# A linear-attention stream that ran inside the first of two layers' iterations is laid over both layers, two iterations to a block of 128 tokens

## What is computed

```python
# linear attention ("mix"): 16 heads of 32
vp = ln(x) @ W_in;  v, p = split(vp);  q = ln(x) @ Wq + bq;  k = ln(x) @ Wk + bk
q = softmax(q);  k = softmax(k);  k = (1 - smear) * k + smear * k_prev      # k_prev: the token before
attn = tril((q / s) @ (k / s).T * decay);  o = attn @ v / (attn.sum(-1) + eps)
s_out = ln(silu(p) * o @ W_out)
# two layers of windowed attention (8 heads of 64, windows of 128) and a gated MLP
h = shift_token(x);  q, k, v = split(h @ wqkv)
q, k = rotary(l2norm(q), l2norm(k));  x = x + softmax(q k^T over this window and the last) v @ wo
h = ln(shift_token(x));  a, g = split(h @ w1 + b1);  x = x + (a * gelu(g)) @ w2 + b2
# end: silu of the second layer's output times s_out, plus x
```

## Time and profile before

| | |
|---|---|
| median of 3 runs | 2132.61 us (2131.91 to 2133.89) |
| profiled execution: time, span | 2133.59 us, 2131.8 us |
| PE busy, DVE busy | 1949.6 us, 1823.7 us |
| ACT busy, POOL busy | 1148.5 us, 935.3 us |
| granted TensorE clock, mean | 0.983 |

### The profile page before, as it was taken

One profiled execution on the slowest core, in us unless ns is written; L12 is line 12 of the kernel. 1 busy time (PEld: TensorE's weight loads), 2 busy tenths in 40 slices (PEclk: granted clock), 3 DMA queues, 4 the chain that ended last, 5 costly groups with the idle time before them and its releaser, 6 DMA issues.

```text
span 2131.8 us, 48702 instructions
## 1 busy us (share of the span) xinstructions
PE 1949.6 (91%) x15282; PEld 1672.7 (78%) x15282; DVE 1823.7 (86%) x5354; ACT 1148.5 (54%) x2734; POOL 935.3 (44%) x941
## 2 busy tenths in 40 slices
PE   4889999989989999999999999899999999999997
PEld 2777878878878778787787887788788788888886
DVE  5688998998998999999899899778888888888884
ACT  2334544544553553554454454656776776676673
POOL 2444554554564465455455455323333333333331
PEclk8799999999999999999999999999999999999998
DMA  5000000000000000000000001121111111111110
GB/s 181 12 15 24 21 18 17 21 20 18 21 20 16 23 20 16 23 20 16 21 17 20 18 22 46 40 70 31 37 37 30 37 36 31 37 33 33 37 29 26
DMA packets 71792, 64.37 MB, mean 30 GB/s; under 512 B 12444, under 2 KB 64984, under 8 KB 71608
## 3 DMA queue, kind: packets, MB, share of 16 engines
q1 hardware_dynamic: 71736, 63.65, 9.9%
HBM read 38.45 MB, written 12.58 MB: 24 GB/s over the span
## 4 chain that ended last, share of the span: by engine, by line
PE 44%; DVE 34%; issue 15%; DMA 3%; ACT 1%; DVEq 1%; SPq 1%; POOL 1%; POOLq 0%; ACTq 0%
PE bank L1327 31%; PE bank L1332 7%; PE bank L1339 5%; DVE prob L942 5%; DVE prob L928 4%; DMA x_shift<-x 3%; DVE rot L1252 3%; DVE sq_sum L1198 2%; DVE qk_sum L1211 2%; DVE rot L1230 2%; DVE hid L1259 1%; DVE state L975 1%; DVE v_mix L1225 1%; DVE h_n L1160 1%; DVE h_n L1158 1%
## 5 line engine op out<-in xcount | busy, mean ns | idle before, releaser
L1327 PE MATMUL bank<-hT_n,w_s 128*128 128x128 f32 x3072 | 390.9, 279 | 0.5 <-ACT hT_n L713 0.5
L1327 PEld LDWEIGHTS bank<-hT_n,w_s 128*128 128x128 f32 x3072 | 366.1, 193 | 15.2 <-issue 10.8
L1332 PE MATMUL bank<-wqkv_s,xT 128*128 128x512 f32 x1152 | 318.8, 412 | 23.7 <-DVE xT L1106 18.5
L743 ACT ACTIVATE prob<-prob,row_min 128x256 f32<-128x256 f32 x512 | 256.1, 503 | 64.4 <-DVE row_min L928 62.0
L1332 PEld LDWEIGHTS bank<-wqkv_s,xT 128*128 128x128 f32 x1152 | 207.4, 191 | 81.7 <-DVE xT L1106 27.0
L942 DVE TENSOR_SCALAR prob<-prob,row_inv 128x256 f32<-128x256 f32 x512 | 224.4, 480 | 9.2
L928 DVE CUSTOM_DVE_ANT_0 prob<-bank,table,inv_norm 128x256 f32<-128x256 f32 x512 | 226.1, 478 | 2.0 <-issue 2.0
L635 POOL TENSOR_TENSOR rot_other<-raw,rot_t 128x256 f32<-128x256 f32 x256 | 186.7, 762 | 93.2 <-ACT raw L713 93.2
L598 POOL TENSOR_TENSOR inv_norm<-sq_clip,half_neg 128x16 f32<-128x16 f32 x64 | 188.7, 2948 | 63.6 <-DVE sq_clip L1201 63.6
L1327 PE MATMUL bank<-w_s,hid 128*128 128x256 f32 x768 | 206.5, 386 | 0.2 <-DVE hid L1259 0.2
L1339 PE MATMUL bank<-table,prob 128*128 128x128 f32 x1024 | 159.7, 279 | 42.6 <-DVE prob L942 40.4
(11 more groups left out here) (182 smaller groups left out, 4361.7 us busy)
## 6 DMA issues: line engine op xcount, KB each, us to landing
k_prev<-k_carry SPq DMA_DIRECT2D x32, 224.0 KB, 2.5
x_s<-in_L_attn_x SPq DMA_DIRECT2D x32, 128.0 KB, 2.1
rot_s<-in_rotary SPq DMA_DIRECT2D x64, 64.0 KB, 2.0
s_between_passes<-s_out SPq DMA_DIRECT2D x32, 128.0 KB, 1.7
x_between_layers<-x SPq DMA_DIRECT2D x32, 128.0 KB, 1.7
x_s<-x_between_layers SPq DMA_DIRECT2D x32, 128.0 KB, 2.0
xn<-x_between_layers SPq DMA_DIRECT2D x32, 128.0 KB, 2.1
s_out<-s_between_passes SPq DMA_DIRECT2D x32, 128.0 KB, 2.1
```

The lines of the kernel that those rows point to most:

```text
L743: ins = act.activation(prob[:, h, :], prob[:, h, :], ACT.Exp, bias=row_min[:, c:c + 1], scale=-1.0, accum_out=row_sum[:, c:c + 1])
L1327: return pe.matmul(out, lhsT, rhs, start=first, stop=last)
L1332: ins = pe.matmul(out, halved(left[:, a]), halved(right[:, b]), start=first and n == 0, stop=last and n == 2)
```

## The change

The mix is spread over all 64 iterations. `linear(i)` gives three pieces: in an odd iteration `one` (chunk i//2: transposes of the rows, q, k, v, p, softmaxes, smear, transposes of k and q at the iteration's end) and `y` (the last norm's output of the chunk before); in an even one `two` (scores, decays, values, state, output product of the chunk whose `one` ran in the iteration ahead). The normalised rows of all windows are stored to DRAM as they are made (`store_rows`, `xh_d`) and read back a chunk at a time (`x_mix`, in the buffer of `y_n`). Score banks 2 and 3 are now the two `mlp_bank`; `turn_q` and `turn_k` use `proj_bank` in both layers, so every `proj_bank_free` waits for kl; the output projection always uses `att_bank[1]`. POOL's `root` for `inv_norm` stands ahead of the two scalings of k. In layer 1 the closing product works in other buffers, and SP waits for the last store of it ahead of loading `x_in`.

The set-up is in two parts: identity, `wqkv`, rotary scales and the first rows are loaded first, and iteration 0 starts on them; the mix weights are prepared inside iteration 0 (`set_up_mix` on PE behind the v product, `cut_mix` on ACT behind the square and on DVE at the iteration's end), and the first chunk's transposes, in iteration 1, wait for the end of it (`mlp_cols`). `fold` writes to `mlp_bank[0]`.

```diff
+        def linear(i):
+            odd, n = i.c == 1, i.low // 2
+            return (Chunk(i.k, n) if odd and n < NW else None,
+                    Chunk(i.k - 1, n - 1) if not odd and 1 <= n < NW + 1 else None,
+                    Chunk(i.k - 1, n - 1) if odd and 1 <= n < NW + 1 else None)
...
-        score_bank = [mix_bank[0], mix_bank[1], att_bank[0], att_bank[2]]
+        score_bank = [mix_bank[0], mix_bank[1], mlp_bank[0], mlp_bank[1]]
...
+            def store_rows(n):
+                sp.wait_ge(norm_dve.sem, norm_dve.at("xh", n))
+                sp.dma_start(xh_d[row(n), :], xh[:, :]).then_inc(xh_stored, 16)
...
+                if i.c == 0 and i.low < UNITS:
+                    c = Chunk(i.k, i.low // 2)
+                    sp.wait_ge(xh_stored, 16 * (c.number() + 1))
+                    sp.dma_start(x_mix[:, :], xh_d[rows, :]).then_inc(xmix_loaded, 16)
...
# POOL, body
+                if two is not None:
+                    pool.wait_ge(mix_act.sem, mix_act.at("qt", two))
+                    pool.tensor_tensor(qT_dec[:, :, :], qT_mix[:, 0:MG // 2, :], query_decay,
...
# DVE, body (layer 0 and 1)
+                if two is not None:
+                    dve.wait_ge(mix_pool.sem, mix_pool.at("gate", two))
+                    decay_scores(two, 3)
                 if a is not None:
                     weigh("a1", a)
+                if two is not None:
+                    decay_scores(two, 2)
+                if a is not None:
                     weigh("b0", a)
...
+                if a is not None:
                     scores("b1", a, att_bank[0])
+                if two is not None:
+                    decay_scores(two, 0)
+                    dve.wait_ge(mix_pool.sem, mix_pool.at("kdec", two))
+                    decay_scores(two, 1)
...
+                if i.low == 0:
+                    cut_mix()
...
# PE, body
+                if one is not None:
+                    pe.wait_ge(xmix_loaded, 16 * (one.number() + 1))
+                    if one.low == 0:
+                        pe.wait_ge(setup_dve.sem, setup_dve.at("mlp_cols", ONCE))
+                    transposes(mix_bank[0], [x_mix[:, c * P:(c + 1) * P] for c in range(DC)])\
...
                 if a is not None:
                     pe.wait_ge(att_act.sem, att_act.at("tb1", a))
                     pe.wait_ge(att_dve.sem, att_dve.at("la", a))
                     att_values("b", a, att_bank[1])
+                if u is not None:
+                    turn_q(u)
+                if m is not None:
+                    hidden(m, mlp_bank[0], 2, 4, 2).then_inc(mlp_pe.done("ga"), 1)
+                    mlp_out(m, 0, 2)
+                if a is not None:
+                    out_projection(a, att_bank[1])
```

More of the change, by code:

```diff
@@ L761, in body @@
             def body(i):
-                mix, proj, a, m, f = streams(i)
+                proj, a, m, f = streams(i)
+                one, two, y = linear(i)
                 if i.low in QKV_CUT:
```

681 lines of the change are left out of this document (334 added, 347 removed).

## The result

The changed kernel takes **2190.02 us** (median of 4 runs, 2189.73 to 2191.0) against 2132.68 for the kernel before (4 runs): ratio **1.0269**, 95% interval 1.0251 to 1.0287. It is slower, by 57 us; I had said 2109 and a range up to 2165. The sign and the range are wrong.

What follows compares the result with a forecast made beforehand. PE was taken to lead, DVE close behind. 110 to iteration 3, 920 to iteration 31, 1021 for 32 to 63, 12 for the change of layers and 46 at the end gave 2109 to 2110 us; range 2055 to 2165.

Steps and rivals of the forecast that it cites:

- the second of the new waits: Even iterations: PE waits for decays standing among DVE's weighings; 1.05 us together, bounds 0 and 1.6.
- step (4): Layer 1's odd iterations: closing product ahead of weigh b1 costs PE 1.3 us, bounds 0.6 and 3; iteration 31.2.
- the work of PE in the base: Layer 1's iteration of 22.94 us, less 0.49 and about 0.5 of waits: 21.9, with xT's 0.36 still in it.
- The check against 15.5: PE's mix work: 7.0 + 8.6 = 15.6 us against 37.44 - 21.97 = 15.5 from the old windows.
- (1) `turn_q`: Query transposes wait for ACT's copy of v: 1.0 us in every iteration of both layers, kept at 0.7 to 1.1.
- (3) layer 0's odd iterations: DVE is the longer engine there: 30.9 us an iteration, bounds 29.9 and 31.7.
- POOL's order: Root ahead of k's scalings: 1.7 us less for weigh b1, later steps meet scalings and gate; counted as equal.
- the third: Rival: DVE bounds odd iterations, weigh b1 meeting a scaling of k on POOL, + 1.7 each; 2163 us, chance 0.25.
- The second rival: Waits between PE and DVE go as well: a pair of iterations takes 61.9 us, total 2053; chance 0.22.
- The fourth: Rival: POOL's root holds DVE's weigh b1, 2.3 us in each odd iteration; 2180 us, chance 0.03.
- The fifth: Rival: the set-up's second part eats the start's gain, first chunk at up to 56; 2121 to near 2128, chance 0.08.
- The signs of being wrong: Weigh b1 showing 2 us, PE's wait on kl at the turn passing 1.8, or a pair under 62.5.

Runs made afterwards that it cites:

- other: Changed kernel, with POOL's rot_other held in even iterations until DVE's third pair of decays is done: 2149.8 us against 2190.
- close: Changed kernel, with POOL's rot_other held in odd iterations of layer 1 until DVE's closing product ends: 2177.6 us against 2190.
- weighp: Changed kernel, with p's addition right behind b1's scores and weigh b1 ahead of the softmax sums in odd iterations: 2179.8 us against 2190.
- turnq: Changed kernel, with the MLP's last gate matmuls ahead of the query transposes on PE: 2149.1 us against 2190.
- klturn: The turnq kernel, with the low half of k (kl) also ahead of norm3 on DVE: 2140.4 us against 2149.
- root: Changed kernel, with POOL's root of the 16 norms again behind the two scalings of k: 2242.1 us against 2190.
- fold: Changed kernel, with fold ahead of the mix scores and its DVE part ahead of weigh a0 in iteration 34: 2182.0 us against 2190.
- best: Changed kernel with turnq, other, kl ahead of norm3, and weighp in layer 1 only: 2077.9 us, ratio 0.9748 to the kernel before.
- decay: Changed kernel, with the first pair of decays ahead of weigh a0 on DVE in even iterations: 2192.3 us against 2190.

## Why the prediction was wrong

**The step that failed** is the second of the new waits, the walk through even iterations ("Walking both engines from the iteration's start"), with its 1.05 between bounds of 0 and 1.6. It took the weighings at their short length and looked for POOL in odd iterations only. The decays put ahead of and between weighings moved a1's and b0's to where POOL has `rot_other`, and they became 1.15 and 1.39. The waits for decays and probabilities came to 0.72 + 0.38 + 0.57 = 1.67. `other` shows the cause: with the meeting away the two later waits vanish, even iterations fall to 32.9, and 40 us go. The trace before held the warning, b0's 1.09 at 1706.39, and the prediction did not look for it.

**The second failure** is the step (4), odd iterations of layer 1. The price of the closing product was 1.3, bounds 0.6 and 3; it is 2.04 of wait, and behind six of 15 such waits 1.55 more at half clock. The mechanism and place were named, the price was too small, in part for the same reason. The 1.3 is the three instructions at their length beside nothing (1.26). In the kernel before they already took 0.82, 0.84 and 0.42, and beside POOL's subtraction and `rot_other` they now take 3.2. With `rot_other` away (`close`) 0.47 of the wait goes; what the subtraction adds no run took away. `weighp` and `close` each took the half clock away with the wait made shorter.

**The third failure** is the work of PE in the base. My pair has 28.5 + 30.1 = 58.7 us of it, yet the earlier trace rows have 59.4, and the changed kernel has 59.44. I took 0.99 of waits off an iteration of 22.94 in which PE idles 0.97 in all, and then left the 0.36 for xT in it as well. The check against 15.5 compared only the mix's part, so it could not find this.

How the 80 are made up, worked out from the means: about 25 from PE's work in 30 even iterations (0.8 each), 19 from their waits (0.6 each), 6 from the four at the low clock, 17 from layer 1's odd iterations, 10 from the start, 9 from the change of layers and 6 from the tail, less 10 in layer 0's odd iterations, where I had DVE as longer than it was (82, rounding apart). The 40 of `other` are therefore not half of the miss: the two waits that vanish there include 0.65 that my 1.05 had counted.

Point by point for the rest:
- *`one`*: PE is busy for 28.5 in odd iterations, as in my sum (28.9 less 0.36). *`two`*: PE is busy for 31.0 in even ones against 30.1. Its pieces, start to start, take 8.8 instead of 8.6; the other 0.6 is not in them, and no run says where in the iteration it lies. The walk's 0.33 for a decay is its start to start (613.20 and 613.53), while the row that I named says 0.41.
- *(1) `turn_q`*: 1.0 predicted, 1.05 measured in both layers. Right, and `turnq` shows that it lay on the path everywhere but in layer 0's odd iterations. I wrote that DVE gets time by it; only there did the time show.
- *(3) layer 0's odd iterations*: 30.9 predicted, 30.2 measured, and DVE as the longer engine was right: `turnq` gained nothing there until kl moved ahead of norm3 (`klturn`, 1.0 each).
- *POOL's order*: I counted the root's move as equal. It is worth 52 us (`root`), 0.9 in an odd iteration of layer 0 and 2.5 in one of layer 1, 1.65 of it the wait. The sum hardly missed it, since the base iteration had weigh b1 at 0.61; the sentence that called the two orders equal was wrong.
- *The start*: the first q product at 12.3 (13 predicted), kl near 36 (34), the first chunk's transposes at 45.0 (44). Right. Iteration 1 was put at 32 and took 41.4: its clock is 0.78 on average, and PE waits 3.28 for the weighing of b1 and 3.00 for kl there. This is 9.4 of the 10.5.
- *The change of layers* was kept at 12; it costs 21.2. `fold` wrote to `proj_bank` before; in `mlp_bank[0]` it waits 5.05 for the decays to read the bank and then runs at the low clock. `fold` takes 5.9 of the 9.2 off iteration 34. *The tail*: 52.0 instead of 46. I had put most of the 8.6 of `two` into a wait of 4.4 for h. PE is busy for 8.1 us longer there, and still waits 4.95 for h, so `two` came on top. No run tests it.
- *The rivals*: the third, DVE as the bound through a meeting with POOL, had the right cause at the wrong place. Its place (weigh b1 at a scaling of k) stayed free (0.62 in both layers), and its sign came true at two places that I hadn't looked at. The second rival (the waits go as well, 61.9 a pair) did not happen by itself; `best` reached its figure, 61.2 and 62.2, by another way, as it takes the 1.0 at `turn_q` away, which that rival kept. The fourth (the root holds DVE) fell: weigh b1 started 0.54 behind the root and took 0.62 (654.81). The fifth fell too, with the first chunk at 45.0.
- *The signs of being wrong*: none of the three came (weigh b1 0.62, the wait on kl 0.59, the pair 64.4). All asked about places that I had already thought of, and none about an even iteration's weighings.

What stays open: where the last 0.7 for the transposes of h could go (`decay` only shows that its neighbour's order doesn't matter), why the clock falls in some even iterations of one order and not of another, where PE's 0.6 more in even iterations lies, what the subtraction costs the closing product, and iteration 1 and the tail.

## What to carry to other kernels

When work is laid out anew, list for each DVE instruction between SBUF tiles what POOL will be doing at its new time, not only whether it stands in a new order; a walk with durations from the old trace is a walk with the old neighbours. Look first at all rows of the same kind in that trace: one that is longer than the rest (1.09 beside 0.62) names the neighbour. And check a summed-up base against the busy time of the old window before adding waits to it. A POOL step that nothing waits for soon can be held back by a semaphore of DVE's, and here one such wait was worth 2%. Where one engine waits at a copy, put independent work that is already late in the order ahead of it, but look first which engine ends the iteration: the wait moves there whole where that one is longer.

## What the runs showed of the hardware

- A DVE multiplication between SBUF tiles, beside a POOL multiplication or subtraction between SBUF tiles, is stretched, and by how much depends on where they meet: the weighing 0.62 to 1.09, 1.15, 1.39 and 2.29; the closing product's instructions 0.42 to 0.84 and 1.54 (`other`, `root` and `close` take such a meeting away or bring it back). POOL's side stretches too: `rot_other` takes 2.77 in `other` and 3.34 beside the closing product.
- DVE instructions that read a PSUM bank and an SBUF table (decays, 0.41) beside the same POOL work keep their length, as does the reduction of 128x1024 (1.21, at 1524.52). Beside POOL's root a product of two SBUF tiles (1.21) and a weighing (0.62, at 654.81) keep theirs.
- The granted clock falls to 1.2 GHz behind PE's wait of 2.04 us in six of 15 odd iterations of layer 1, in all where that wait is 3.6 to 3.7 (`root`), and in none where it is 1.57 (`close`) or gone (`weighp`). A fall costs 1.5 us, but nothing where waits for DVE follow it (`weighp`, 33.92 with the clock at 0.95). Why six and not all, no run shows.
